# Moving a batch of small matmuls behind the value product, and four tiny steps of a scale chain into PSUM

## Chip, core and metric

One core of a Trainium2 chip. The metric is the device time of one execution in microseconds (us), as the median of several runs. The engines are TensorE (PE; PEld is its weight load), VectorE (DVE), ScalarE (ACT), GpSimd (POOL), and SyncE (SP), which here issues the DMAs. SBUF is the working memory, PSUM holds the results of matmuls in eight banks of 128 partitions by 512 floats.

## What is computed

Two layers over x of shape (4, 1024, 512), with a condition vector of 128 numbers per batch element:

```python
# layer 0: gated feed-forward, FF = 2048, down projection on quantised values
h = x * ((cond @ norm_w.T + 1) * rsqrt(mean(x * x) + 1e-6))
val, gate = split(h @ up_w.T)                    # up_w is (4096, 512)
h = val * gelu(gate)
scale = 127 / clip(max(abs(h), axis=-1), 1e-5)   # one per token
hq = round(h * scale) / scale
x = hq @ ternary(down_w).T + x
# layer 1: adapter whose weights depend on the condition
Wd_b = Wd + 0.1 * (cond @ Wdd.T + bdd)           # Wdd is (65536, 128); the same for Wu_b
x = x + relu(x @ Wd_b.T + bd) @ Wu_b.T + bu
```

The layer-1 weights come from `Wdd` and `Wdu`, two matrices of 65536 x 128 floats that are read from HBM. Everything the kernel does with them besides loading is called the delta work here.

## The kernel before

**Chunks and slots.** The 4096 tokens are handled as 8 chunks c = 0 to 7 of 512 tokens. A chunk has 16 slots j = 0 to 15, one per 128 rows of the feed-forward dimension. Every engine runs its own program of these 128 slots, and semaphores tie them together. There is no planner: the order of work within a slot is written out by hand in each engine's `run(c, par, b)`.

**A slot on PE** (L1302 to L1348) is a gate product (12 matmuls of 128x128 by 128x512, L1176 to L1178, into bank `GATE[j % 2]`), then a value product (12 more, into `VAL[j % 2]`), with other work placed between the two or behind both. In slot 0 of every chunk but the first, `turn_absrun` (L1264) stands between them and `spread_scales` (L1270) behind them. In slots 9 to 12, `down_products` (16 matmuls, L1280, into bank `Y`) multiply the quantised values of the chunk before. `down_products(c, t)` for t > 0 waits for `y_done`, the DVE's `residual` (L968) of row block t - 1, because there is only one bank `Y`. A value product waits for `max_done`: the DVE must have taken the running maximum (L905) of the slot two before, whose bank it reuses.

**A slot on the other engines.** ACT computes gelu of the gate bank (L696), after the DVE's product with the value bank (`h`, L1013) its absolute value into the VAL bank (L710), and in slots 0 to 7 the rounding of the chunk before (`round_pair`, L671 and L674). The DVE runs in this order: `finish_max` and `quantise` (L878) of the chunk before, the running maximum of the slot before (L905), `residual`, `turn_units`, `sum_part` (L909), then `h` (L1013), then the normalisation of the next chunk's x (`scale_x` L855, `x_lower` L860). In slot 0, `turn_units` stands between `finish_max` and `quantise`.

**The delta work.** The upper and lower parts of `Wdd` and `Wdu` go two ways. POOL multiplies, and adds up in two steps, 64 parts (L564, L567, L571), which the DVE finishes (`sum_part`, L909). The rest is 96 units. For each, SP loads two tiles of 128x512 (`load_nat`, L384), the DVE transposes them (`turn_nat`, L895) into one of four places of `natT`. Four units make a batch m, and PE multiplies it with `delta_products(m)`: 16 matmul instructions (32 records in the trace, L1235) into bank `HY`. There is one `natT`: the DVE's first transposes of a batch wait until PE has finished the batch before (`delta_mm`). After every second batch ACT copies `HY` out (`read_sums`, L685), and SP stores it (`store_stage`, L388).

**When units and batches come.** `unit_slots` gives one unit to a slot, two to slots 9 to 12, and leaves one unit out in the slot behind the end of a batch. `batch_at(c, j)` puts a batch's delta products into the slot behind its last unit. So in 18 of 24 cases the slot with the delta products has no unit of its own. In six (slot 10 of chunk 1, slot 11 of chunks 2 to 6) it has one, since one of two is left. The 18 are slots 1, 6 and 13 of chunk 1, slots 2, 7 and 14 of chunk 2, and slots 3, 8 and 14 of chunks 3 to 6. Twelve of these 18 have an odd m, so that `read_sums` and `store_stage` follow: slots 6 and 13 of chunk 1, 7 and 14 of chunk 2, 8 and 14 of chunks 3 to 6.

**From the maximum to the scales.** `finish_max(c)` runs in slot 0 of the next chunk: a reduction of bank `TB` to four numbers per partition (`m4`, L864), a lower bound (`mc`, L866), a reciprocal (`rs`, L868), a product with 127 (`s4`, L870), and a factor for later (`fy`, L871). PE waits for `s4` before `spread_scales` writes it to bank `TB` for the quantisation. The DVE's `mean_square` (L842) is another such small step elsewhere.

**SP's queue** is in order too. In slot j it holds, among others: the transposing loads of the next chunk's x (L344, L349), `load_nat`, `load_part`, loads of x for the residual and stores of x1, and last `store_stage`.

Of the kernel before, what the change touches and what calls it, by code (L numbers as in the profile page):

```python
# [5 lines left out]
F32 = mybir.dt.float32  # L6
# [5 lines left out]
ALU = mybir.AluOpType  # L12
ACT = mybir.ActivationFunctionType
AX = mybir.AxisListType

P = 128
# [9 lines left out]
def conditioned_block(nc, x, cond, norm_w, up_w, down_w, Wd, bd, Wu, bu, Wdd, bdd, Wdu, bdu, out):  # L26
# [6 lines left out]
    NCH = N // CH  # L33
    TT = CH // P
# [19 lines left out]
    with ExitStack() as ctx:  # L54
        def sb(name, shape, dt):
            return ctx.enter_context(nc.sbuf_tensor(name, shape, dt))

        def sem(name):
            return ctx.enter_context(nc.semaphore(name))
# [43 lines left out]
        ss = sb("ss", [P, TT], F32)  # L103
        rstd = sb("rstd", [P, TT], F32)
        mhalf = sb("mhalf", [P, TT], F32)
        m4 = sb("m4", [P, TT], F32)
        mc = sb("mc", [P, TT], F32)
        rs = sb("rs", [P, TT], F32)
        s4 = sb("s4", [P, TT], F32)
        fy = sb("fy", [P, TT], F32)  # L110
        wabs = sb("wabs", [P, 2 * TT], F32)
        unused = sb("unused_gelu", [P, 1], F32)
        wtot = sb("wtot", [P, 4], F32)
# [29 lines left out]
        bank = [ctx.enter_context(nc.psum_tensor(f"bank{i}", [P, 512], F32)) for i in range(8)]  # L143
        GATE, VAL = [bank[0], bank[1]], [bank[2], bank[3]]
        Y, HY, TA, TB = bank[4:8]


        def upn(jj, i):
# [22 lines left out]
        def halves_done(jj, p):  # L171
            return 2 * jj + p + 1 if jj < SPLIT else SPLIT + jj + 1
# [16 lines left out]
        def first_bank(c, k):  # L189
# [32 lines left out]
        absrun_turned, max_read, scale_step, s_turned = (sem(n) for n in (  # L222
            "absrun_turned", "max_read", "scale_step", "s_turned"))
# [39 lines left out]
        def row_in(c, j):  # L263
            return c + 1 < NCH and ((is_first(c) and j == 4) or (c % 2 == 1 and j == 6))
# [19 lines left out]
        def is_first(c):  # L284
            return c == 0
# [23 lines left out]
        def units_at(c, j):  # L309
            return unit_slots.get(FT * c + j, [])  # L310

        def batch_at(c, j):
            return [u // NATT for u in unit_slots.get(FT * c + j - 1, []) if u % NATT == NATT - 1]
# [491 lines left out]
        def _(dve):  # L805
# [54 lines left out]
                dve.tensor_tensor(xn_lo[:, t, :], xn[:, t, :], xn_hi[:, t % 2, :], ALU.subtract).then_inc(x_lo_done, 1)  # L860

            def finish_max(c):
                dve.wait_ge(absrun_turned, c + 1)
                dve.tensor_reduce(m4[:, :], TB[:, :].rearrange("p (t f) -> p t f", t=TT), AX.X, ALU.max).then_inc(max_read, 1)  # L864
                dve.wait_ge(max_read, c + 1)
                dve.tensor_scalar(mc[:, :], m4[:, :], 1e-5, None, ALU.max).then_inc(scale_step, 1)  # L866
                dve.wait_ge(scale_step, 4 * c + 1)
                dve.reciprocal(rs[:, :], mc[:, :]).then_inc(scale_step, 1)  # L868
                dve.wait_ge(scale_step, 4 * c + 2)
                dve.tensor_scalar(s4[:, :], rs[:, :], 127.0, None, ALU.mult).then_inc(scale_step, 1)  # L870
                dve.tensor_scalar(fy[:, :], mc[:, :], wtot[:, 3:4], None, ALU.mult).then_inc(scale_step, 1)  # L871

            def quantise(c, k0):
                if k0 == 0:
# [266 lines left out]
        def _(pe):  # L1141
# [31 lines left out]
            def up_products(par, ft, bank, done):  # L1173
                cols = slice(ft * P, (ft + 1) * P)
                for k in range(KD):
                    pe.matmul(bank[:, :], w_hi[:, k, cols], xh[:, par, k, :], start=(k == 0), stop=False)  # L1176
                    pe.matmul(bank[:, :], w_hi[:, k, cols], xl[:, par, k, :], start=False, stop=False)  # L1177
                    mm = pe.matmul(bank[:, :], w_lo[:, k, cols], xh[:, par, k, :], start=False, stop=(k == KD - 1))  # L1178
                mm.then_inc(done, 1)
# [48 lines left out]
            def delta_products(m):  # L1228
                pe.wait_ge(nat_turned, 8 * m + 8)
                if m % 2 == 0:  # L1230
                    pe.wait_ge(stage_full, m // 2 + 1)
                cols = slice(256 * (m % 2), 256 * (m % 2) + 256)
                for a in range(HB):
                    for t in range(4):
                        mm = pe.matmul(HY[32 * t:32 * t + 32, cols], cond_diag[:, a, :], natT[:, (4 * m + t) % NATT, :, a, :],  # L1235
                                       start=(a == 0), stop=(a == HB - 1))
                mm.then_inc(delta_mm, 1)

            def turn_delta_down(b):
                pe.wait_ge(delta_back[b], 16 * 8)  # L1240
                if b == 0:
                    pe.wait_ge(stage_full, GROUPS + 1)
                    pe.wait_ge(h_scaled, FT * (NCH - 1))
                else:
                    pe.wait_ge(layers_ready, 2 * b - 1)
                for k in range(KD):
                    mm = pe.transpose(HY[:, k * P:(k + 1) * P], delta_d[:, b, k * P:(k + 1) * P], identf[:, :])
                mm.then_inc(delta_turned, 1)
# [8 lines left out]
            def turn_absrun(c):  # L1257
                pe.wait_ge(max_done, FT * (c + 1))
                if c > 0:
                    pe.wait_ge(h_scaled, FT * c)  # L1260
                if c == NCH - 1:
                    pe.wait_ge(layers_ready, 2 * NB)
                for t in range(TT):
                    mm = pe.transpose(TB[:, t * P:(t + 1) * P], absrun[:, t * P:(t + 1) * P], identf[:, :])  # L1264
                mm.then_inc(absrun_turned, 1)

            def spread_scales(c):
                pe.wait_ge(scale_step, 4 * c + 3)
                for t in range(TT):
                    mm = pe.transpose(TB[:, t * P:(t + 1) * P], s4[:, t:t + 1].to_broadcast([P, P]), identf[:, :])  # L1270
                mm.then_inc(s_turned, 1)
# [22 lines left out]
            def run(c, par, b):  # L1294
                first, last = is_first(c), b is None

                if not first:
                    for i in range(2):
                        pe.wait_ge(x_hi_turned[i], 32 * c)
                    pe.wait_ge(x_turned, 16 * TT * c)  # L1300
                    pe.wait_ge(h_done, FT * c - 1)
                for j in range(FT):  # L1302
                    n = FT * c + j
                    if first and j == 0:
                        first_products()
                        continue
                    if first:
                        pe.wait_ge(w_lo_done, halves_done(j, 0))
                    if not (first and j < 2):
                        pe.wait_ge(gelu_done, n - 1)  # L1310
                    up_products(par, FT + j, GATE[j % 2], gate_full)
                    if not first and j == 0:
                        turn_absrun(c - 1)
                    for m in batch_at(c, j):
                        delta_products(m)
                    if last and 10 <= j < 14:
                        turn_delta_down(j - 10)
                    if first and j in (2, 3):
                        if j == 2:
                            pe.wait_ge(base_done, 2)  # L1320
                        pe.wait_ge(ta_freed, TA_BASE + j - 2)
                        for k in range(KD):
                            mm = pe.transpose(TA[:, k * P:(k + 1) * P], base[2 * (j - 2)][:, k * P:(k + 1) * P], identf[:, :])
                        mm.then_inc(ta_full, 1)
                    if first and j + 2 < FT:
                        turn_w(j + 2)
                    if not (first and j < 2):
                        pe.wait_ge(max_done, n - 1)
                    if first:
                        if j < SPLIT:  # L1330
                            pe.wait_ge(w_lo_done, halves_done(j, 1))
                        else:
                            pe.wait_ge(value_turned[j % 2], 32 * ((j - SPLIT) // 2 + 1))
                    up_products(par, j, VAL[j % 2], val_full)
                    if first and j == 8:
                        pe.wait_ge(mean_step, 1)
                        pe.wait_ge(ta_freed, TA_MEAN)
                        pe.matmul(TA[:, 0:1], ones[:, :], wtot[:, 0:1], start=True, stop=True).then_inc(ta_full, 1)
                    if last and 10 <= j < 14:
                        turn_delta_up(j - 10)  # L1340
                    if not first and j == 0:
                        spread_scales(c - 1)
                    if row_in(c, j):
                        spread_row(b)
                    for i in pairs_turned(c, j):
                        turn_pieces(i)
                    if not first and 9 <= j < 9 + TT:
                        down_products(c - 1, j - 9)  # L1348
# [173 lines left out]
```

## Time and profile before

| | us |
|---|---|
| median of 3 runs | 940.36 (938.34 to 940.86) |
| the profiled execution | 937.38 |
| its span, first to last instruction | 935.2 |
| outside the span | 2.2 |
| busy: PE 921.9, PEld 452.1, DVE 687.5, ACT 427.2, POOL 646.0 | |

The span is what the trace covers. A matmul of 512 columns is shown with a length of 0.38 us, though the next one starts 0.216 us later: their ends are modelled and overlap. So a PE pause shows as idle time only where it is longer than that overlap. To find pauses one compares the starts of neighbours. "c6 j14" below is slot 14 of chunk 6.

### The profile page before, as it was taken

The numbers are of one execution on the slowest core, as the hardware profiler recorded it, in microseconds if no ns is written. First come the engines' busy times: TensorE is split into PE (matmuls) and PEld (weight loads), VectorE is DVE, ScalarE is ACT, GpSimd is POOL, SyncE is SP. The second block draws the span as 40 slices with busy tenths as digits, with TensorE's granted clock in tenths as the row PEclk, the third lists the DMA queues.
The fourth block names the chain that finished last, engine by engine and source line by source line (L and its number), as shares of the span: only waits on it lengthen the run. The fifth ranks groups of instructions, "written<-read, shape, count | busy, mean of one in ns | idle before, by whom it ended". The sixth has DMA issues, their size and how long they took to land.

```text
span 935.2 us, 13874 instructions
## 1 busy us (share of the span) xinstructions
PE 921.9 (99%) x5002; PEld 452.1 (48%) x5002; DVE 687.5 (74%) x1034; ACT 427.2 (46%) x788; POOL 646.0 (69%) x565
## 2 busy tenths in 40 slices
PE   9999999999999999999999999999999999999997
PEld 6555544444444444444444444444444444455586
DVE  6778778867878678776878688686878665356676
ACT  7897667214742157123742257222751156215343
POOL 1000049899979998799988999799987999200664
PEclk9999999999999999999999999999999999999999
DMA  9999644655446553574346552584446526020584
GB/s 310 224 229 209 178 138 144 160 156 158 121 133 158 159 152 97 159 196 135 122 121 199 157 161 88 152 212 113 143 116 183 142 68 180 12 74 29 198 296 179
DMA packets 142059, 144.04 MB, mean 154 GB/s; under 512 B 51876, under 2 KB 89256, under 8 KB 141480
## 3 DMA queue, kind: packets, MB, share of 16 engines
q1 hardware_dynamic: 141992, 143.17, 53.7%
q8 instruction: 39, 0.64, 0.3%
q14 instruction: 28, 0.23, 0.1%
HBM read 112.46 MB, written 19.92 MB: 142 GB/s over the span
## 4 chain that ended last, share of the span: by engine, by line
PE 70%; POOL 8%; DVE 7%; issue 5%; DMA 5%; ACT 3%; SPq 2%; DVEq 0%; POOLq 0%; ACTq 0%
PE bank L1176 17%; PE bank L1178 17%; PE bank L1177 17%; POOL delta_reg L564 4%; PE bank L1280 4%; PE bank L1235 4%; DVE delta_reg L895 3%; POOL delta_reg L567 2%; DMA xr<-in_x 2%; DMA delta_reg<-in_L_cond_Wdd 2%; PE bank L1290 1%; POOL delta_reg L571 1%; PE bank L1417 1%; PE bank L1426 1%; PE bank L1447 1%
## 5 line engine op out<-in xcount | busy, mean ns | idle before, releaser
L564 POOL TENSOR_TENSOR delta_reg<-delta_reg,s_bc 128x512 f32<-128x512 f32 x256 | 334.3, 1327 | 91.7 <-DMA delta_reg<-in_L_cond_Wdu 78.7
L1176 PE MATMUL bank<-x_split,w_hi 128*128 128x512 f16 x1016 | 385.3, 379 | 0.9 <-DVE absrun L905 0.9
L1178 PE MATMUL bank<-x_split,w_lo 128*128 128x512 f16 x1016 | 385.1, 379 | 0.0
L1177 PE MATMUL bank<-x_split,w_hi 128*128 128x512 f16 x1016 | 385.1, 379 | 0.0
L710 ACT ACTIVATE bank<-h 128x512 f32<-128x512 f32 x126 | 75.7, 601 | 309.0 <-DVE h L1013 308.9
L895 DVE STREAM_TRANSPOSE delta_reg<-delta_reg 128x512 f32<-128x512 f32 x192 | 197.1, 1107 | 24.6 <-DMA delta_reg<-in_L_cond_Wdd 18.7
L567 POOL TENSOR_TENSOR delta_reg<-delta_reg 128x512 f32<-128x512 f32 x128 | 166.7, 1302 | 10.0
L1013 DVE SCALAR_TENSOR_TENSOR h<-bank,desc,g 128x512 f32<-128x512 f32 x128 | 94.7, 740 | 99.9 <-issue 54.7
L1176 PEld LDWEIGHTS bank<-x_split,w_hi 128*128 128x128 f16 x1016 | 99.4, 98 | 123.0 <-issue 8.2
L1178 PEld LDWEIGHTS bank<-x_split,w_lo 128*128 128x128 f16 x1016 | 99.4, 98 | 119.9
L1177 PEld LDWEIGHTS bank<-x_split,w_hi 128*128 128x128 f16 x1016 | 99.4, 98 | 112.1
L696 ACT ACTIVATE g<-bank,desc 128x512 f32<-128x512 f32 x128 | 87.2, 681 | 90.4 <-PE bank L1178 90.4
L571 POOL TENSOR_TENSOR delta_reg<-delta_reg 128x256 f32<-128x256 f32 x128 | 94.5, 738 | 47.9 <-DVE delta_reg L909 39.0
L1280 PE MATMUL bank<-wqT,qreg 128*128 128x512 fp8e4 x448 | 101.3, 379 | 0.8 <-DVE xr L968 0.8
L905 DVE TENSOR_TENSOR absrun<-bank,absrun 128x512 f32<-128x512 f32 x118 | 80.8, 684 | 21.4 <-ACT bank L710 21.4
L671 ACT ACTIVATE h<-h 128x512 f32<-128x512 f32 x112 | 65.0, 623 | 40.7 <-DVE h L878 40.7
L878 DVE TENSOR_TENSOR h<-h,bank 128x512 f32<-128x512 f32 x112 | 71.4, 678 | 0.6 <-PE bank L1270 0.6
L1280 PEld LDWEIGHTS bank<-wqT,qreg 128*128 128x128 bf16 x448 | 43.6, 98 | 53.7 <-DVE xr L968 2.3
L674 ACT ACTIVATE qreg<-h 128x512 bf16<-128x512 f32 x112 | 63.6, 617 | 0.0
L607 POOL TENSOR_TENSOR out_own<-xn,sc_row 128x512 f32<-128x512 f32 x8 | 10.1, 1290 | 71.9 <-DVE h L1120 69.4
L968 DVE SCALAR_TENSOR_TENSOR xr<-bank,fy,xr 128x512 f32<-128x512 f32 x30 | 22.2, 744 | 39.6 <-issue 27.0
L1235 PE MATMUL bank<-delta_reg,cond_diag 128*32 128x256 f32 x768 | 46.4, 382 | 3.2 <-DVE delta_reg L895 3.1
(182 smaller groups left out, 754.6 us busy)
## 6 DMA issues: line engine op xcount, KB each, us to landing
delta_reg<-in_L_cond_Wdd SPq DMA_DIRECT2D x128, 256.0 KB, 2.9
delta_reg<-in_L_cond_Wdu SPq DMA_DIRECT2D x128, 256.0 KB, 3.2
qreg<-in_L_cond_up_w SPq DMA_DIRECT2D x32, 256.0 KB, 4.7
xr<-in_x SPq DMA_DIRECT2D x30, 256.0 KB, 4.2
x_scratch<-xr SPq DMA_DIRECT2D x30, 256.0 KB, 4.1
xn<-in_x SPq DMA_DIRECT2D x7, 1024.0 KB, 6.1
h<-in_L_cond_down_w SPq DMA_DIRECT2D x4, 1024.0 KB, 7.8
delta_reg<-in_L_cond_down_w SPq DMA_DIRECT2D x8, 512.0 KB, 4.6
```

The lines of the kernel that those rows point to most:

```text
L564: pool.tensor_tensor(part_mul[:, b, :, :], part_w[:, i % 2, :, :], cond_all[:, 2 * pair + b, :].unsqueeze(1).to_broadcast([P, 4, C]), ALU. ...
L567: pool.tensor_tensor(part_mul[:, :, :, 0:64], part_mul[:, :, :, 0:64], part_mul[:, :, :, 64:128], ALU.add).then_inc(part_step, 1)
L571: pool.tensor_tensor(part_low[:, i % 2, 2 * pair:2 * pair + 2, :, :], part_mul[:, :, :, 0:32], part_mul[:, :, :, 32:64], ALU.add).then_inc ...
L696: act.activation(g[:, j % 2, :], GATE[j % 2][:, :], ACT.Gelu, scale=desc[:, 2 * j + 1:2 * j + 2]).then_inc(gelu_done, 1)
L895: dve.transpose(natT[:, t, k, :, :].rearrange("p a (r e) -> p e a r", e=4), nat[:, v % HALVES, :]).then_inc(nat_turned, 1)
L905: dve.tensor_tensor(absrun[:, :], abs_tile(c, j), absrun[:, :], ALU.max).then_inc(max_done, 1)
L1013: dve.scalar_tensor_tensor(h[:, j, :], VAL[j % 2][:, :], desc[:, 2 * j:2 * j + 1], g[:, j % 2, :], ALU.mult, ALU.mult).then_inc(h_done, 1)
L1176: pe.matmul(bank[:, :], w_hi[:, k, cols], xh[:, par, k, :], start=(k == 0), stop=False)
L1177: pe.matmul(bank[:, :], w_hi[:, k, cols], xl[:, par, k, :], start=False, stop=False)
L1178: mm = pe.matmul(bank[:, :], w_lo[:, k, cols], xh[:, par, k, :], start=False, stop=(k == KD - 1))
L1235: mm = pe.matmul(HY[32 * t:32 * t + 32, cols], cond_diag[:, a, :], natT[:, (4 * m + t) % NATT, :, a, :], start=(a == 0), stop=(a == HB - 1))
L1280: mm = pe.matmul(Y[:, :], q[:, f, t * P:(t + 1) * P], wqT[:, f, :], start=(f == 0), stop=(f == FT - 1))
```

## The change

Two things. `m4`, `mc` and `rs` move from SBUF into the first 12 columns of PSUM bank `Y`, except for the last chunk, where a tile in SBUF stays. `s4` and `fy` stay in SBUF. In PE's slot, the delta products go behind the value product (and behind `spread_scales`, ahead of `spread_row`, `turn_pieces` and `down_products`) where the slot has no unit. The six batches in slots with a unit stay between gate and value product.

```diff
-        m4 = sb("m4", [P, TT], F32)
-        mc = sb("mc", [P, TT], F32)
-        rs = sb("rs", [P, TT], F32)
+        scale_tiles = sb("scale_tiles", [P, 3 * TT], F32)
...
+        def scale_tile(c, i):
+            return (scale_tiles if c == NCH - 1 else Y)[:, TT * i:TT * (i + 1)]
...
             def finish_max(c):
+                m4, mc, rs = (scale_tile(c, i) for i in range(3))
                 dve.wait_ge(absrun_turned, c + 1)
-                dve.tensor_reduce(m4[:, :], TB[:, :].rearrange("p (t f) -> p t f", t=TT), AX.X, ALU.max).then_inc(max_read, 1)
+                dve.tensor_reduce(m4, TB[:, :].rearrange("p (t f) -> p t f", t=TT), AX.X, ALU.max).then_inc(max_read, 1)
                 dve.wait_ge(max_read, c + 1)
-                dve.tensor_scalar(mc[:, :], m4[:, :], 1e-5, None, ALU.max).then_inc(scale_step, 1)
+                dve.tensor_scalar(mc, m4, 1e-5, None, ALU.max).then_inc(scale_step, 1)
                 dve.wait_ge(scale_step, 4 * c + 1)
-                dve.reciprocal(rs[:, :], mc[:, :]).then_inc(scale_step, 1)
+                dve.reciprocal(rs, mc).then_inc(scale_step, 1)
                 dve.wait_ge(scale_step, 4 * c + 2)
-                dve.tensor_scalar(s4[:, :], rs[:, :], 127.0, None, ALU.mult).then_inc(scale_step, 1)
-                dve.tensor_scalar(fy[:, :], mc[:, :], wtot[:, 3:4], None, ALU.mult).then_inc(scale_step, 1)
+                dve.tensor_scalar(s4[:, :], rs, 127.0, None, ALU.mult).then_inc(scale_step, 1)
+                dve.tensor_scalar(fy[:, :], mc, wtot[:, 3:4], None, ALU.mult).then_inc(scale_step, 1)
...
                     up_products(par, FT + j, GATE[j % 2], gate_full)
                     if not first and j == 0:
                         turn_absrun(c - 1)
-                    for m in batch_at(c, j):
-                        delta_products(m)
+                    if units_at(c, j):
+                        for m in batch_at(c, j):
+                            delta_products(m)
...
                     if not first and j == 0:
                         spread_scales(c - 1)
+                    if not units_at(c, j):
+                        for m in batch_at(c, j):
+                            delta_products(m)
                     if row_in(c, j):
                         spread_row(b)
```

## Rows read from the trace of the kernel before

**Rows 1.** The page: busy times; then PE's granted clock in 40 slices.
```profile
PE 921.9 (99%) x5002; PEld 452.1 (48%) x5002; DVE 687.5 (74%) x1034; ACT 427.2 (46%) x788; POOL 646.0 (69%) x565
...
PEclk9999999999999999999999999999999999999999
```

**Rows 2.** Waits of PE, whole span: line <- who; us in total, times, longest.
```profile
PE bank L1235 <- DVE delta_reg L895: 3.1, 8, 0.7
...
PE bank L1280 <- DVE xr L968: 0.8, 2, 0.6
...
PE bank L1270 <- DVE s L870: 0.4, 2, 0.3
```

**Rows 3.** Timeline of PE ahead of delta products: start, length; c2 j7, then c6 j14.
```profile
261.99 0.38 PE L1178 MATMUL bank<-x_split,w_lo 128*128 128x512 f16 x1
262.29 0.85 PE L1235 MATMUL bank<-delta_reg,cond_diag 128*32 128x256 f32 x12
...
741.94 0.38 PE L1178 MATMUL bank<-x_split,w_lo 128*128 128x512 f16 x1
742.88 1.93 PE L1235 MATMUL bank<-delta_reg,cond_diag 128*32 128x256 f32 x32 [0.56 <-DVE delta_reg L895]
```

**Rows 4.** Timeline of PE ahead of the spread of scales, c4 j0 and c7 j0.
```profile
437.48 0.38 PE L1177 MATMUL bank<-x_split,w_hi 128*128 128x512 f16 x1
437.70 0.38 PE L1178 MATMUL bank<-x_split,w_lo 128*128 128x512 f16 x1
438.36 0.65 PE L1270 MATMUL bank<-identf,s 128*128 128x128 f32 x4 [0.28 <-DVE s L870]
...
757.93 0.38 PE L1178 MATMUL bank<-x_split,w_lo 128*128 128x512 f16 x1
758.39 0.65 PE L1270 MATMUL bank<-identf,s 128*128 128x128 f32 x4
```

**Rows 5.** Timeline of DVE, `finish_max` in c4 j0.
```profile
435.53 0.69 DVE L864 TENSOR_REDUCE m<-bank 128x4 f32<-128x512 f32 x1 [0.86 <-PE bank L1264]
436.25 1.26 DVE L866 TENSOR_SCALAR mc<-m 128x4 f32<-128x4 f32 x1
...
437.76 0.55 DVE L870 TENSOR_SCALAR s<-rs 128x4 f32<-128x4 f32 x1
```

**Rows 6.** Timeline of POOL beside it.
```profile
436.22 1.27 POOL L567 TENSOR_TENSOR delta_reg<-delta_reg 128x512 f32<-128x512 f32 x1
```

**Rows 7.** Instructions by line: durations ns min/median/max, first and last start us.
```profile
L866 DVE TENSOR_SCALAR mc<-m x8: 169/272/1259, 114.9 to 857.0; 128x4 f32<-128x4 f32 x8
...
L870 DVE TENSOR_SCALAR s<-rs x8: 170/554/1097, 115.3 to 857.4; 128x4 f32<-128x4 f32 x8
```

**Rows 8.** Groups by line, xcount | busy us, mean ns | idle before us.
```profile
L905 DVE TENSOR_TENSOR absrun<-bank,absrun 128x512 f32<-128x512 f32 x118 | 80.8, 684 | 21.4 <-ACT bank L710 21.4
L710 ACT ACTIVATE bank<-h 128x512 f32<-128x512 f32 x126 | 75.7, 601 | 309.0 <-DVE h L1013 308.9
...
L1065 DVE TENSOR_SCALAR sc<-bank 128x16 f32<-128x16 f32 x1 | 0.2, 169 | 0.0
```

**Rows 9.** Timeline of PE, the value product of c1 j3.
```profile
133.72 0.39 PE L1176 MATMUL bank<-x_split,w_hi 128*128 128x512 f16 x1 [0.93 <-DVE absrun L905]
```

**Rows 10.** Timeline of DVE ahead of that.
```profile
130.30 1.57 DVE L886 TENSOR_SCALAR xr<-delta_reg 128x1024 bf16<-128x1024 f32 x1
```

**Rows 11.** Timeline of DVE, c6 j8 and j9.
```profile
697.34 0.75 DVE L1013 SCALAR_TENSOR_TENSOR h<-bank,desc,g 128x512 f32<-128x512 f32 x1 [3.68 <-PE bank L1178]
...
705.70 1.10 DVE L895 STREAM_TRANSPOSE delta_reg<-delta_reg 128x512 f32<-128x512 f32 x1 [2.95 <-DMA delta_reg<-in_L_cond_Wdd]
```

**Rows 12.** Timeline of ACT in c6 j8.
```profile
699.78 0.58 ACT L685 ACTIVATE stage<-bank 128x512 f32<-128x512 f32 x1
```

**Rows 13.** Timeline of SP's issues, c6 j8.
```profile
700.39 0.33 SPq L388 DMA_DIRECT2D delta_scratch<-stage  x1
```

**Rows 14.** Timeline of PE, down products of c6 j10.
```profile
711.69 0.39 PE L1280 MATMUL bank<-wqT,qreg 128*128 128x512 fp8e4 x1 [0.63 <-DVE xr L968]
```

## Prediction

> **What bounds the kernel now.** I read the busy line and the granted clock first: PE is busy 99% of the span at full granted clock, the DVE 74%, POOL 69% [rows 1]. So only three things could shorten the run: less work for PE, a faster PE, or fewer pauses of it. The change keeps every matmul, and the clock has nothing to give. What is left is PE's pauses, and the next view to read is who made PE wait [rows 2]: the delta products waited for the DVE's transposes 8 times, 3.1 us; the spread of the scales for `s4` twice, 0.4 us; the down products for the residual twice, 0.8 us. One value product waited for the running maximum, 0.93 us [rows 9].
>
> These idle times are too small, because a matmul is drawn 0.38 us long while its successor starts earlier. In the timeline I take starts instead. Two neighbouring matmuls of a product start 0.22 us apart [rows 4]. From the last gate matmul to a delta product it takes 0.30 us where nothing is awaited, and 0.94 us in c6 j14, a true pause of 0.64 where the idle column says 0.56 [rows 3]. So I add 0.08 to each pause before delta products, and 0.38 - 0.22 = 0.16 to each pause before the spread or the down products.
>
> **The delta products behind the value product.** Nothing is removed: the same 18 batches of 1.93 us [rows 3] run in the same slot, with one change to and one from this kind of matmul each, as before. What moves is the moment at which the transposes are needed. A value product of 12 matmuls takes 12 x 0.22 = 2.6 us. The longest wait is 0.7 us [rows 2], so the value product covers each of the eight, by at least 1.9 us. The value product itself does not start to wait: the running maximum that it needs stands ahead of the transposes in the DVE's order, one slot before, so where PE now waits for the transposes, that maximum is done.
>
> What is late next? PE arrives earlier at the value product of the slot after next, whose maximum needs the DVE's `h`. In seven of the eight cases the DVE gets there in time: after the last transpose it has a sum, `h`, in slots below 8 the quantisation and the maximum, some 4 us, against 2.6 + 1.9 + 2.6 us of PE. The eighth is c1 j1, 0.7 us. There, the value product of c1 j3 starts at 133.72 after a wait of 0.93 [rows 9], for a DVE that was busy until 131.87 with a step on the pieces of `down_w` that took 1.57 [rows 10]; this chain comes from ACT and hangs on none of PE's products of slot 1. An earlier PE waits 0.7 longer there. That case gives nothing. The others: 3.1 - 0.7 = 2.4, plus 7 x 0.08 = 0.56, together **3.0 us**.
>
> **What the move does to those behind.** `natT` comes free later. After the value product's end the DVE must do `h` (0.75 [rows 11]), ACT the absolute value (0.60), the DVE the maximum (0.68 [rows 8]), 2.0 us and the gaps between them, before it comes to the next transposes; the delta products end about 1.9 us after the value product. Cost 0, with 0.1 to 0.3 us to spare; without that cover it is at most 1.9 us of DVE time per batch, in a DVE that idles 26% of the span. ACT's `read_sums` waits for the delta products, with the next gelu queued behind it, but this gelu needs the next gate product, 2.6 us later. On SP, `store_stage` waits for `read_sums`, and the next slot's transposing load and `load_nat` are queued behind it.
>
> That last queue decides a further gain. In c6 j8, `h` waits for PE until 697.34 after 3.68 us of idleness [rows 11], then come `read_sums` at 699.78 [rows 12], the store at 700.39 [rows 13] with the transposing load and the `load_nat` behind it, and at 705.70 a transpose that waited 2.95 us for its DMA [rows 11]. So the DVE is late in slot 9, and at 711.69 PE has waited 0.63 us for a residual [rows 14]. With the value product ahead of the delta products, `h` of slot 8 comes 1.9 to 2.2 us earlier, the delta products end where the value product ended, at about 697.3, and `read_sums` can start then, more than 2 us before its 699.78. The whole chain up to the residual moves forward by about 2 us, and the pause goes: 0.63 + 0.16 = **0.8 us**. (The other wait of this kind, 0.2, is in chunk 1, with no moved batch near: 0.)
>
> **The scale steps in PSUM.** L866 and L870 work on four numbers and should take 0.17 us, their minimum; their maxima are 1259 and 1097 ns [rows 7]. In c4 j0, L866 starts at 436.25 and ends at 437.51 [rows 5], and POOL's add over SBUF starts at 436.22 and ends at 437.49 [rows 6]: the small step ends when POOL's does. Out of the eight boundaries the seven that change lose up to 2 x 1 us each. A step with PSUM as its source takes 169 ns (L1065 [rows 8]), but with POOL idle then. The Trainium skill, page "SBUF — State Buffer", section "Who interferes with whom", gives the reason: a `tensor_scalar` between SBUF and SBUF uses the port pair that it shares with GpSimd, an exclusive lock; with at most one SBUF operand on its own port it doesn't contend. Rows 5 and 6 agree as to the waiting. Against the change speaks the skill's page "VectorE: DVE Perf Modes", in its section on the TRN2 errata, with a fixed cost of 120 cycles out of PSUM against 58 in SBUF: by that 65 ns more for each step, 0.2 us on the way to `s4`, an estimate, and the sum would be the same.
>
> Writes of the DVE into PSUM have no row. Bounds from rows: 0.17 us as in SBUF, and 0.69 us, the reduction out of PSUM over 512 columns [rows 5]. I take 0.17, by the step of nearest size. Then `s4` comes in c4 at 435.53 + 0.69 + 3 x 0.2 = 436.9 and not 438.3. PE would want it at 437.70 + 0.22 = 437.92, so 1 us remains, and the pause goes: 438.36 - 437.70 - 0.22 = 0.44. In c7 0.46 - 0.22 = 0.24 [rows 4]; the second of the two waits for `s4` in rows 2, in c2, has 0.4 - 0.28 = 0.12 of idleness, plus 0.16: 0.3. Together **1.0 us**. The other 5 us or so that the DVE saves fall where it isn't late for PE, and show nowhere. At the upper bound three steps cost 2.1 us, `s4` comes at 438.4, and this gain is 0.
>
> **The sum.** 3.0 + 0.8 + 1.0 = 4.8 us of PE's pauses. PE has no long wait elsewhere that could take them back [rows 2]; the DVE waits for PE at `h` in every chunk, so that it follows an earlier PE. Against the profiled execution, 937.4 (span 935.2 and 2.2 outside), that is 932.6. That execution lies 3.0 below the median of the runs, 940.36; taking 4.8 from the median gives **935.6 us**.
>
> **Rivals.**
> *Taken back in the same chunk.* In slots 9 to 13 DVE, SP and DMAs work in a chain that wakes PE late even now [rows 14]. If it doesn't follow, the lead from slots 0 to 3 is lost in slot 10 (as c1 j1's is in j3), and the 0.8 isn't won. Then the spread (c7's 0.24) and the delta pauses of slot 14, about 1.4, remain, up to 2 or 3: 937.5 to 939. For it: the 0.6 us waits there. Against: the chain begins with an `h` that waited 3.68 us for PE [rows 11].
> *The change doesn't do what it says in `s4`.* L870 still writes SBUF. If that alone makes it wait, only L866 gets shorter. Even so, in c4 it saves 1.1 us of a pause of 0.44, though POOL may then hold L870 longer: loss up to 1.0, 936.6.
> *Slower.* The mechanism is SP's queue in slot 8: if `store_stage` came later than now, by as much as the batch is moved, 2.2 us, then load, transposes and residual of slots 9 and 10 do too. The pause of slot 10 is already there in c6; taking chunks 3 to 5 to be as close to it, some 4 x 2 = 8 us would be lost and the 4.0 of the other two terms (less c6's 0.8, never won) kept: 940.4 + 8 - 4 = 944. It decides from the point at which `read_sums` starts later than now, that is over 2.5 us after the end of the delta products, as 699.78 stands against 697.3. I see nothing to cause that.
>
> **How the numbers follow.** The forecast (3.8 to 6 us faster) gets 0.62, the rival that takes back 0.18, the one of `s4` 0.06, slower 0.04, no change at all 0.05 (the pauses move to where I don't look), and more than 6 us 0.05 (the DVE's saved time helps further). What a measurement of this kernel can tell from no change is about 0.3%, 2.8 us. Faster than that: 0.62 + 0.06 + 0.05 and a few hundredths of the second case, 0.75. Within it: 0.21. Slower: 0.04. The range runs from 6.5 + 1 of scatter below the median, 932.9, to the less gained of the taken-back case, 939.0.
>
> **What would show it.** Right: no row of PE's waits for L1235 or `s`; L866 and L870 at 0.17 to 0.25 us in chunks 0 to 6, and L870 after the last chunk as before; the pause of c1 j3 grown from 0.93 to about 1.65; in c6 the store of slot 8 at least 2 us nearer to the slot's start. Wrong: new rows of PE waiting for the running maximum or the residual in chunks 2 to 6; transposes that wait for L1235 in most of the slots after a moved batch; a PSUM step over 0.5 us.

## The result: 0.6% faster, and the profile after

| | median us | against the kernel before, interval |
|---|---|---|
| before | 938.18 (7 runs) | |
| after | 932.37 (7 runs) | 0.9938 [0.9921, 0.9955] |

That is 5.8 us (by the interval 4.2 to 7.4), where 4.8 were forecast, and a median 3.2 us below the forecast one, just outside the range that began at 932.9. One of the seven runs of after was slow, 965.8 us at a granted clock of 0.949, and the ratio leaves it out. The profiled execution of after took 932.4, its span is 930.2.

The page of after, busy times:

```profile
PE 921.0 (99%) x5002; PEld 453.6 (49%) x5002; DVE 684.4 (74%) x1034; ACT 429.1 (46%) x788; POOL 645.6 (69%) x565
```

The instruction counts are those of [rows 1], and no engine's busy time differs by more than 3.1 us. The difference is in who made PE wait (columns as in [rows 2]; the lines of PE that matter here are numbered 3 higher than before, those from L1353 on 7 higher):

```profile
PE bank L1360 <- POOL identb L549: 1.9, 1, 1.9
PE bank L1179 <- DVE absrun L908: 1.5, 1, 1.5
PE bank L1463 <- ACT down_hi L782: 0.6, 1, 0.6
PE bank L1159 <- DVE qreg L823: 0.4, 1, 0.4
```

The waits of the delta products (L1235, now L1238), of the spread (L1270, now L1273) and of the down products (L1280, now L1283) in [rows 2] are gone. One wait is longer than in [rows 9], that of the value product in c1 j3, L1179. PE's timeline and the DVE's there:

```profile
132.54 0.38 PE L1181 MATMUL bank<-x_split,w_lo 128*128 128x512 f16 x1
134.40 0.39 PE L1179 MATMUL bank<-x_split,w_hi 128*128 128x512 f16 x1 [1.49 <-DVE absrun L908]
```

```profile
132.47 1.27 DVE L881 TENSOR_TENSOR h<-h,bank 128x512 f32<-128x512 f32 x2
133.67 0.68 DVE L908 TENSOR_TENSOR absrun<-bank,absrun 128x512 f32<-128x512 f32 x1
```

The scale steps, by line (durations min/median/max, then first and last start), against [rows 7]:

```profile
L869 DVE TENSOR_SCALAR bank<-bank x7: 170/171/171, 115.8 to 751.9; 128x4 f32<-128x4 f32 x7
```

```profile
L873 DVE TENSOR_SCALAR s<-bank x7: 161/161/161, 116.2 to 752.3; 128x4 f32<-128x4 f32 x7
L873 DVE TENSOR_SCALAR s<-scale_tiles x1: 170/170/170, 852.5 to 852.5; 128x4 f32<-128x4 f32 x1
```

Maxima of 1259 and 1097 ns have become 171 and 161. And POOL was busy beside most of them. In c4 j0, L869 starts at 435.10, while the first of these was running:

```profile
434.41 0.73 POOL L573 TENSOR_TENSOR delta_reg<-delta_reg 128x256 f32<-128x256 f32 x1
435.22 2.50 POOL L566 TENSOR_TENSOR delta_reg<-delta_reg,s_bc 128x512 f32<-128x512 f32 x2
```

L873 runs at 435.53, in the midst of a POOL product that began at 435.22, and takes 0.16 us.

**A ruler for the traces.** PE's whole steady part lies between the first reduction ahead of the scales and the last. In the trace shown of before these start at 114.2 and 856.3, 742.1 us apart. In after:

```profile
L867 DVE TENSOR_REDUCE bank<-bank x7: 694/700/700, 115.0 to 751.1; 128x4 f32<-128x512 f32 x7
L867 DVE TENSOR_REDUCE scale_tiles<-bank x1: 691/691/691, 851.4 to 851.4; 128x4 f32<-128x512 f32 x1
```

851.4 - 115.0 = 736.4, 5.7 us less. What follows the last reduction is as long in both (78.9 and 78.8 us). I call the stretch between the two reductions the steady part below, and a *pause* the distance between the starts of two neighbouring PE matmuls less what it is where nothing is awaited (0.22, or 0.31 before delta products). Over the steady part, before has pauses of 7.3 us in 17 places, after a single one of 1.65.

### The profile page after: what moved, and what is told of

It reads as the page before. It is cut to its first block, busy times and chain, and to the rows that moved or that the text cites. A ratio compares the mean times of both kernels' runs of the same rounds, so it can differ in the third digit from the quotient of the medians.

```text
span 930.2 us, 13874 instructions
## 1 busy us (share of the span) xinstructions
PE 921.0 (99%) x5002; PEld 453.6 (49%) x5002; DVE 684.4 (74%) x1034; ACT 429.1 (46%) x788; POOL 645.6 (69%) x565
## 4 chain that ended last, share of the span: by engine, by line
PE 94%; ACT 2%; DVE 2%; DMA 1%; issue 1%; SPq 0%; DVEq 0%; ACTq 0%
PE bank L1179 23%; PE bank L1180 23%; PE bank L1181 23%; PE bank L1283 10%; PE bank L1238 5%; PE bank L1293 1%; PE bank L1424 1%; PE bank L1433 1%; PE bank L1159 1%; PE bank L1454 1%; PE bank L1456 1%; PE bank L1455 1%; PE bank L1463 1%; DMA xn<-in_x 1%; PE bank L1464 1%
## 5 line engine op out<-in xcount | busy, mean ns | idle before, releaser
L566 POOL TENSOR_TENSOR delta_reg<-delta_reg,s_bc 128x512 f32<-128x512 f32 x256 | 329.4, 1308 | 90.4 <-DMA delta_reg<-in_L_cond_Wdu 77.2
L1179 PE MATMUL bank<-x_split,w_hi 128*128 128x512 f16 x1016 | 385.3, 379 | 1.5 <-DVE absrun L908 1.5
L1179 PEld LDWEIGHTS bank<-x_split,w_hi 128*128 128x128 f16 x1016 | 99.4, 98 | 123.2 <-issue 9.5
L573 POOL TENSOR_TENSOR delta_reg<-delta_reg 128x256 f32<-128x256 f32 x128 | 98.5, 769 | 43.1 <-DVE delta_reg L912 34.5
L1283 PE MATMUL bank<-wqT,qreg 128*128 128x512 fp8e4 x448 | 101.3, 379 | 0.0
L1283 PEld LDWEIGHTS bank<-wqT,qreg 128*128 128x128 bf16 x448 | 43.9, 98 | 52.2
L1238 PE MATMUL bank<-delta_reg,cond_diag 128*32 128x256 f32 x768 | 46.4, 382 | 0.0
```

The costliest lines, as they stand in the source:

```text
L566: pool.tensor_tensor(part_mul[:, b, :, :], part_w[:, i % 2, :, :], cond_all[:, 2 * pair + b, :].unsqueeze(1).to_broadcast([P, 4, C]), ALU. ...
L573: pool.tensor_tensor(part_low[:, i % 2, 2 * pair:2 * pair + 2, :, :], part_mul[:, :, :, 0:32], part_mul[:, :, :, 32:64], ALU.add).then_inc ...
L1283: mm = pe.matmul(Y[:, :], q[:, f, t * P:(t + 1) * P], wqT[:, f, :], start=(f == 0), stop=(f == FT - 1))
```

## Experiments

The line numbers in the expectations are those of the changed kernel, unless said otherwise.

**e1: the changed kernel again.** No edit.

> The changed kernel once more, on the same chip as its two halves. Theory: it is faster by PE's pauses alone. Compared from the reduction ahead of chunk 0's scales (L864 in the trace of the kernel before, at 114.2) to the one after chunk 7 (856.3), that is 742.1 us before and 736.3 in the first trace of after; expected again 736.3 within 0.2, and the time 5 to 6 us below the kernel before. If the 1 us more than the 4.8 of the forecast was scatter of the start or of the median, the stretch would be 737.3 in a second trace.

931.97 us, ratio 0.9937 [0.9921, 0.9954], 5.9 us below the kernel before by the ratio and 6.5 by the medians; steady part 735.9 (first reduction at 114.4, last at 850.3). So the steady part of the first trace of after was no exception. The 0.2 of tolerance was too tight: the pause of c1 j3 was 1.1 here, and 1.9 in a third trace (e11). It follows the first of the DVE's two long steps in front, L885:

```profile
129.04 0.69 DVE L885 TENSOR_SCALAR delta_reg<-delta_reg 128x1024 f32<-128x1024 f32 x1 [2.36 <-ACT delta_reg L682]
```

```profile
128.66 1.60 DVE L885 TENSOR_SCALAR delta_reg<-delta_reg 128x1024 f32<-128x1024 f32 x1 [2.36 <-ACT delta_reg L682]
```

The first is e1, where POOL was idle at its start, the second e11. In after it took 1.22. Wherever POOL was busy at its start, it ended 0.55 us after POOL's instruction did. The second long step took 1.57 in all three.

**e2: only the move.**

```diff
-            return (scale_tiles if c == NCH - 1 else Y)[:, TT * i:TT * (i + 1)]
+            return scale_tiles[:, TT * i:TT * (i + 1)]
```

> Only the delta products are moved; m4, mc and rs stay in SBUF. Theory (the parts add, each by its own pauses): no pause before delta products, none at the down products, but pauses at the spread of scales stay, some 1.0 to 1.3 us in 3 to 5 of the 7 boundaries, so 1.0 to 1.3 us longer than e1: 4.4 to 4.8 faster than before. Rival (PSUM steps save DVE time that matters further on too): over 2 us longer than e1.

932.68 us, ratio 0.9941 [0.9926, 0.9956], 0.7 us above e1. The steps wait again, and PE with them twice (0.34 us in c2 j0, 0.39 in c5 j0 by starts), not at the boundaries c4 and c7 of [rows 4]:

```profile
L873 DVE TENSOR_SCALAR s<-scale_tiles x8: 169/558/1098, 115.5 to 853.2; 128x4 f32<-128x4 f32 x8
```

```profile
PE bank L1273 <- DVE s L873: 0.4, 2, 0.2
```

So the pauses at the spread come back with SBUF, but in two boundaries and 0.7 us, less than the 1.0 to 1.3 in three to five that I expected: which boundaries lose time changes from execution to execution. The steady part, 737.7, is 1.7 longer than in e1, and 1.0 of that is the pause of c1 j3 (2.14 for 1.13), which varies as much between traces of the changed kernel.

**e3: only the PSUM steps.**

```diff
-                    if units_at(c, j):
-                        for m in batch_at(c, j):
-                            delta_products(m)
+                    for m in batch_at(c, j):
+                        delta_products(m)
...
-                    if not units_at(c, j):
-                        for m in batch_at(c, j):
-                            delta_products(m)
```

> Only the scale steps are in PSUM; all delta products stay between gate and value product. Theory: the spread's pauses go, 1.0 to 1.2 us; the DVE comes 0.6 to 1.5 us earlier to slots 1 to 3 of chunks 2 to 6, so that the pauses before delta products in slots 2 and 3 (0.7, 0.4, 0.3 and 0.4 us in chunks 2, 4, 5, 6) go too, by this half as well: together 2.8 to 3.0 us faster than before. Those of slots 13 and 14 (1.3 us together) and of the down products stay. Rival (the halves share nothing, as the forecast's sum has them): 1.0 us faster, with the pauses of slots 2 and 3 in place.

934.81 us, ratio 0.9966 [0.9951, 0.9982]: 3.2 us faster (by the interval 1.7 to 4.6), which fits the theory's 2.8 to 3.0 and excludes the 1.0 that my sum gave this half. PE's waits for transposes:

```profile
PE bank L1238 <- DVE delta_reg L898: 1.7, 3, 1.0
```

Eight such waits have become three, in c1 j1, c2 j14 and c6 j14. Those of slots 2 and 3 of chunks 2, 4, 5 and 6 went without any batch being moved, because the DVE came out of `finish_max` earlier. At c2 j14 the pause even grew, from 0.25 to 1.05. The transposes there stand behind a residual that waited for its load of x:

```profile
313.78 0.75 DVE L971 SCALAR_TENSOR_TENSOR xr<-bank,fy,xr 128x512 f32<-128x512 f32 x1 [4.01 <-DMA xr<-in_x]
```

The down products kept their pauses, as expected: 1.05 us in c6 j10, 0.20 in c4 j10 and 0.12 in c6 j12.

So the halves give 5.5 and 3.2 alone and 5.9 together (1 minus the ratios of e2, e3 and e1, times 938.5): they cure partly the same pauses.

**e4: the batches of slots 7 and 8 stay.**

```diff
-                    if units_at(c, j):
+                    if units_at(c, j) or j in (7, 8):
...
-                    if not units_at(c, j):
+                    if not (units_at(c, j) or j in (7, 8)):
```

> The changed kernel, but the batches of slots 7 and 8 stay between gate and value product (5 of the 18 moved ones; none of these had a pause of its own). Theory (their move pulls the chain h, read_sums, store, loads, transposes, residual of slots 8 to 10 forward by 2 us): store_stage of c6 j8 comes about 2 us later against the slot's gate product than in the changed kernel, and PE waits for a residual in slot 10 or 11 of some chunks again, 0.1 to 1.0 us in all; 0.3 to 1.0 us longer than e1. Rival (the pause at the down products went for another reason, the scales or the earlier slots 2 and 3): no such wait, the time of e1 within 0.2.

935.06 us, ratio 0.9951 [0.9933, 0.9969], against 0.9937 for e1. The intervals overlap, so the times don't settle this; the traces have to. The down products wait again:

```profile
PE bank L1283 <- DVE xr L971: 0.5, 2, 0.3
```

By starts these are pauses of 0.28 us in c4 j10 and 0.49 in c6 j10, and a third of 0.36 in c1 j12, 1.1 together. SP's issues of c6 j8, in e4 and then in after:

```profile
699.95 0.33 SPq L390 DMA_DIRECT2D delta_scratch<-stage  x1
700.32 1.21 SPq L346 DMA_TRANSPOSE x_split<-xn_hi  x1
```

```profile
695.02 0.33 SPq L390 DMA_DIRECT2D delta_scratch<-stage  x1
695.39 1.21 SPq L346 DMA_TRANSPOSE x_split<-xn_hi  x1
```

and PE's delta products of this slot, first e4, then after:

```profile
691.97 1.93 PE L1238 MATMUL bank<-delta_reg,cond_diag 128*32 128x256 f32 x32
```

```profile
692.02 1.93 PE L1238 MATMUL bank<-delta_reg,cond_diag 128*32 128x256 f32 x32
```

In e4 a value product of 2.6 us still follows them, so the slot ends at 696.4, and the store comes 3.5 us behind its end. In after the slot ends with them at 693.9, and the store comes 1.1 us behind. So the chain of the forecast runs 2.4 us earlier in its slot. The pauses of c4 j10 and c6 j10 stand in all three traces of before (0.9 to 1.2 us together), in e3 (1.25) and here (0.8), and in none of the nine traces in which the batches of slots 7 and 8 are behind: a batch that never had a pause of its own cures another one. (The two profiled executions lie 4.0 apart: 1.0 of it are the pauses of the down products, 1.1 is c1 j3, 2.2 against 1.1, and 2.0 lie ahead of the first reduction, 116.4 against 114.4.)

**e5: all 24 batches behind.** The six whose slot has a unit move as well.

```diff
-                    if units_at(c, j):
-                        for m in batch_at(c, j):
-                            delta_products(m)
...
-                    if not units_at(c, j):
-                        for m in batch_at(c, j):
-                            delta_products(m)
+                    for m in batch_at(c, j):
+                        delta_products(m)
```

> The changed kernel with the six remaining batches (slot 10 of chunk 1, 11 of chunks 2 to 6), whose slot has a unit, behind the value product as well. Theory: the DVE's transpose of that slot stands ahead of its h and now waits for delta products that end 2.6 us later; it idles up to 2 us more in each of the six, in the slots in which the DVE is the late one; PE waits for it at the residuals of slots 12 and 13 for up to 1 us each: 1 to 6 us longer than the changed kernel. Rival (DMAs set the pace of slots 9 to 13 and hide it): within 0.5 us of the changed kernel.

936.47 us, ratio 0.9974 [0.996, 0.9987], 4.1 to 4.5 us above after and e1 by the medians, 3.4 by the ratios: six batches give back most of what 18 have won. The DVE's waits for the delta products, then PE's for the residual:

```profile
DVE delta_reg L898 <- PE bank L1238: 21.7, 6, 5.2
```

```profile
PE bank L1283 <- DVE xr L971: 3.0, 4, 1.2
```

There are exactly six waits of the DVE, and by starts PE pauses in slot 12 of all six chunks, 0.92, 0.88, 1.37, 0.54, 0.26 and 0.23 us, 4.2 together. The DVE waits up to 5.2 us, not 2: its chain in slots 9 to 13 runs ahead by then, so that it comes early and waits for the value product of 2.6 us as well, and at most for part of the gate product. (In after there are such waits as well, 7.2 us in five cases, all in slots whose batch stayed; none costs PE anything.) This is a slower case that I hadn't among my rivals, and the condition in the change is what keeps it off.

This trace shows one thing more, in c1 j3. After the pause of 2.15 us, eight matmuls of the value product start 0.43 us apart where 0.22 is usual:

```profile
137.88 0.63 PE L1179 MATMUL bank<-x_split,w_hi 128*128 128x512 f16 x1
138.31 0.63 PE L1180 MATMUL bank<-x_split,w_hi 128*128 128x512 f16 x1
```

The granted clock of the stretch from 136.6 to 139.5 is 0.50, that is the lower level, 1.2 GHz; it cost 1.7 us. In e8 the same follows a pause of 2.20. In e2, e4 and e7 it does not, after 2.12 to 2.18, nor in any trace with a shorter pause. So the pause of c1 j3, which the change makes longer, had a second cost in two traces. Whether the untraced runs with a mean clock of 0.998 (933.9 of after, 934.8 of e1) owe their length to it isn't shown; none of the 39 runs of before in the comparisons is below 0.999.

**e6: the last piece of down_w two slots later**, on top of the change.

```diff
-            return [i for i, slot in enumerate((9, 10, 11, 12, 13, 14, 15, 17)) if slot == FT * c + j]
+            return [i for i, slot in enumerate((9, 10, 11, 12, 13, 14, 15, 19)) if slot == FT * c + j]
...
-            return [i for i, slot in enumerate((10, 11, 12, 13, 14, 15, 16, 20)) if slot == FT * c + j]
+            return [i for i, slot in enumerate((10, 11, 12, 13, 14, 15, 16, 21)) if slot == FT * c + j]
```

> The changed kernel with the last eighth of down_w quantised in slot 3 of chunk 1 and not in slot 1 (and turned in slot 5, not 4). Theory (the pause that slot 1's delta products hand on to the value product of c1 j3, 1.65 us by starts, comes from ACT's and DVE's two long steps on that piece, which wait for POOL): the pause goes or falls below 0.5, and the time by 1.1 to 1.65 us against the changed kernel: 7 us faster than the kernel before. Rival (the DVE is late in chunk 1 anyway, for the first quantisations): the pause moves to slot 5 or so, no gain.

930.55 us, ratio 0.9916 [0.99, 0.9931], 7.9 us faster than before. The steady part is 850.1 - 115.4 = 734.7:

```profile
L867 DVE TENSOR_REDUCE bank<-bank x7: 690/700/700, 115.4 to 749.8; 128x4 f32<-128x512 f32 x7
L867 DVE TENSOR_REDUCE scale_tiles<-bank x1: 691/691/691, 850.1 to 850.1; 128x4 f32<-128x512 f32 x1
```

No pause is left in it. So the pause of c1 j3 came from that piece, and what c1 j1 handed on was to be had after all.

**e7: only m4 in PSUM.**

```diff
-            return (scale_tiles if c == NCH - 1 else Y)[:, TT * i:TT * (i + 1)]
+            return (scale_tiles if c == NCH - 1 or i > 0 else Y)[:, TT * i:TT * (i + 1)]
```

> The changed kernel with only m4 in PSUM, mc and rs in SBUF: L869 reads PSUM and writes SBUF, L873 reads and writes SBUF. Theory (a tensor_scalar waits for POOL only if both its tensors are in SBUF): L869 takes 0.16 to 0.18 us in every chunk, L873 waits as before, 0.5 to 1.1 us in most of chunks 1 to 6. Rival (it is the write to SBUF that waits): L869 waits as well, up to 1.2 us.

By line, L869 (PSUM to SBUF in seven chunks), then L873 (SBUF to SBUF in all):

```profile
L869 DVE TENSOR_SCALAR scale_tiles<-bank x7: 160/161/162, 115.1 to 751.7; 128x4 f32<-128x4 f32 x7
```

```profile
L873 DVE TENSOR_SCALAR s<-scale_tiles x8: 169/330/1065, 115.5 to 852.3; 128x4 f32<-128x4 f32 x8
```

The time was 932.14 us (one run), no pause at the spread. Four of the seven L869 ran wholly inside a POOL instruction. So a source in PSUM suffices; the write to SBUF doesn't wait. My rival about `s4` falls with this, and with L873 in after. The step for `fy`, L874, SBUF to SBUF with a column as factor, waited here twice, for 1.3 us, where I had thought that it never would:

```profile
436.22 1.31 DVE L874 TENSOR_SCALAR fy<-scale_tiles,wtot 128x4 f32<-128x4 f32 x1
```

**e8: a column as factor.**

```diff
-                dve.tensor_scalar(ss[:, :], ss[:, :], 1.0 / D, EPS, ALU.mult, ALU.add).then_inc(ms_done, 1)
+                dve.tensor_scalar(ss[:, :], ss[:, :], inv_d[:, 0:1], EPS, ALU.mult, ALU.add).then_inc(ms_done, 1)
```

> The changed kernel; mean_square (L844, in SBUF) takes its factor from a column in SBUF instead of a constant. It took 1.1 to 1.3 us in chunks 1 to 6, where fy's step, which has such a column, never took more than 0.23 while between SBUF tiles. Theory A (fy's step only never waited because it followed directly on a step that had waited): still 1.1 to 1.3 us. Theory B (with a column as factor the step doesn't need what POOL holds): 0.22 us in every chunk. Either way no change in time beyond 0.3 us, since the DVE isn't late in slot 5.

```profile
L846 DVE TENSOR_SCALAR ss<-ss,inv_d x7: 230/1020/1277, 49.2 to 679.5; 128x4 f32<-128x4 f32 x7
```

932.84 us (one run, with the stretch at half rate named in e5). It waits all the same, so theory B falls: a column as factor doesn't help. But theory A's reason doesn't hold either. In e7 `fy`'s step followed directly on one that had waited and still took 1.3 us, in the two chunks in which POOL's next instruction began 0.02 us after it; where it took 0.22 in the kernel before, that came 0.14 us after it.

**e9 and e10: the kernel before, traced twice more.**

> The kernel before, unchanged, for a second trace of it. Theory (PE's pauses hang on where POOL stands when a short DVE step begins, so they differ from one execution to the next): the floor of a chunk between pauses is the same (105.4 or 105.9 us from one reduction of L864 to the next, less chunk 1), but single pauses differ by up to 1 us from the first trace, and their sum, 7.3 us there, is another by 0.5 to 2 us. Rival (fixed pauses): the same pauses within 0.1 us each, and the scatter of the runs comes from the first 114 us.

> A third trace of the kernel before; the same expectations as for e9. By the theory the sums of the pauses of the three traces differ by over 0.5 us and the first 114 us by 1 to 3 us; by the rival only the latter.

The steady parts, by the reduction of e9 and then of e10, are 740.5 and 739.9 us:

```profile
L864 DVE TENSOR_REDUCE m<-bank x8: 686/692/693, 114.7 to 855.2; 128x4 f32<-128x512 f32 x8
```

```profile
L864 DVE TENSOR_REDUCE m<-bank x8: 684/692/692, 113.9 to 853.8; 128x4 f32<-128x512 f32 x8
```

PE's pauses come to 5.7 and 5.2 us, not 7.3, with another distribution: those of c1 j1 (0.78, 0.69) and c2 j2 (0.71, 0.62) stay, the one of c4 j0 (0.45 in [rows 4]) is missing in both, the one of c6 j10 is 1.13 and 0.92 for 0.79. The first 114 us vary by 0.8. So the pauses are not fixed, and the start scatters by less than the 1 to 3 us that I expected. For the spread the traces show the link with POOL: in c4, L866 and L870 together took 1.81 us in the first trace, with the pause, and 1.07 and 1.22 in e9 and e10, without. For the other pauses the link is argued. The trace on which I built had the largest pauses of three.

**e11 and e12: the changed kernel and e6's on one chip.**

> The changed kernel beside the one with the late piece, on one chip. 1.1 to 2.2 us longer than e12, all of it the pause of the value product of c1 j3.

> The kernel of e6 again. If its 7.9 us against the kernel before hold: 930 to 931 us, no pause of PE over 0.1 us between the first and the last reduction ahead of the scales, 734.7 us apart within 0.2.

931.36 (0.9916 [0.9894, 0.9938]) and 930.94 us (0.9909 [0.9883, 0.9936]). The steady parts differ as expected (736.6 and 735.0; 1.92 us in c1 j3 against nothing there, though 0.29 in c1 j12), the medians only by 0.4, and the two profiled executions not at all (931.8 and 931.7), because e12's first reduction came at 115.7 and e11's at 114.2. The first reductions lie between 113.9 and 114.7 in the three traces of before and between 113.6 and 116.4 in those of the changed kernel and its variants. That e6's edit saves 1.0 to 1.9 us of the steady part is shown (736.4, 735.9 and 736.6 against 734.7 and 735.0); that its median is lower is within the scatter on this chip (1.4 us lower over e1 and e6, 0.4 here).

## Why the prediction was wrong in the number and right in most of its reasons

The forecast missed the median by 3.2 us: 935.6 against 932.4. Two parts:

**The base, 2.2 us.** The step that failed is "taking 4.8 from the median". I took the sum from 940.36, the median of three runs. With four more it was 938.18, and in the later comparisons 938.5 (19 runs), 938.7 (13) and 939.3 (7). The profiled execution, 937.4, was the better base; with it the same sum would have given 932.6. That this meets 932.4 is luck: the base would have been 0.8 too low and the sum 1.0 too small. I allowed 1 us of scatter at the lower end, for three runs that lay 2.5 us apart. This alone put 932.37 outside the range.

**The sum, 1.0 us: 4.8 for 5.8.** Term by term, from the first trace of each kernel:

- *Delta products, 3.0.* The pauses before them were 3.9 by starts and are 0; c1 j3 took back 0.56 (1.09 to 1.65). So 3.3. The forecast counted eight waits of the idle column and missed two below its resolution. Its point on c1 j1, that an earlier PE waits longer in j3 and that the case gives nothing, was right in kind: e6 shows that the long DVE step in front was the cause. It expected "about 1.65" of a column that showed 0.93 before; that column shows 1.49, and 1.65 is the pause by starts. It is a coincidence in any case: e1, e11, e2 and e4 have 1.1, 1.9, 2.1 and 2.2.
- *Down products, 0.8.* 1.3: c4 j10 (0.13) and c1 j12 (0.36) went too. I had put the latter at 0, "with no moved batch near", in after it is gone, in e1 0.11 and in e4 back at 0.36. It scatters, whatever the kernel: 0.29 in e12, and none in e9 and e10. So the 0.36 isn't shown to be the change's doing; the 0.9 of c4 and c6 is (e4).
- *Scales, 1.0.* Right by the first traces, and about 0.15 more inside the three spreads that waited (the sum to `s4` in c4 is 436.8, printed as 436.9). In e9 and e10 the pauses of this term are 0.4 and 0.1. But e2 and e3 show that the term is not this half's own worth, which is 0.4 to 0.7 beside the other half (by the ratios, by the medians) and 3.2 without it. "The other 5 us or so that the DVE saves ... show nowhere" was wrong for this half by itself: the saved time also cures the pauses of slots 2 and 3.

These make 3.3 + 1.3 + 1.15 = 5.7, the difference of the steady parts. Against the three traces of before (740.8 on average) and of after (736.3) it would be 4.5. The two late traces of before, at 936.3 and 934.9 us, lie below all seven runs beside them (936.6 to 941.5). So 4.5 us of the measured 5.8 to 7.9 are located in PE's pauses, and where the other 1.3 to 3.4 lie stays open: in the traces it is neither the start nor the end, and the longer runs of before have no trace.

**The other points.** *Cost 0 of the later `natT`:* right, the DVE waits for delta products in no slot behind a moved batch; but the bound without that cover, "at most 1.9 us of DVE time per batch", doesn't hold where the slot has a unit: in e5 such a wait took up to 5.2. *The chain of slot 8:* right, 2.4 us for "about 2" (e4). *The steps in PSUM:* 0.16 to 0.17 us, the value taken; the upper bound of 0.69 was far off. *The rivals:* the lead was not taken back in slots 9 to 13, since the chain there moved along; `s4` doesn't wait (e7); the slower case through `store_stage` did not come, the store being earlier, not later. There is a slower case, e5's, which the change avoids; I should have priced it, since the condition `units_at` in the diff points at it. "The clock has nothing to give" left out that it can take: e5 and e8 lost 1.7 us to it behind the longer pause of c1 j3.

## What to carry to other kernels

Where PE is 99% busy, look for its pauses by the distance of starts, and let PE do first the work that doesn't have to wait. Check that no other engine has a wait for the postponed work queued ahead of what PE needs from it next: the same edit gains in 18 slots and loses in six. Don't add up two halves of a change before asking whether they cure the same pause. And take the base of a forecast from as many runs as there are, with their spread in the range: here it cost 2.2 us, and the sum 1.0.

## What the runs showed of the hardware

- A `tensor_scalar` of four numbers on the DVE from SBUF to SBUF takes 0.17 us or up to 1.31; wherever it was drawn out, it ended 23 to 29 ns after a POOL instruction did. The Trainium skill, page "SBUF — State Buffer", section "Who interferes with whom", says that this form of instruction can contend for a port pair with GpSimd and that the later one waits, and the traces agree. It holds for a constant and for a column as factor (e7, e8). With the source in PSUM it takes 0.16 us to SBUF and 0.17 to PSUM, whatever POOL does (e7 and after).
- The reciprocal of four numbers never waited, not even between two tiles in SBUF: 177 to 179 ns in all 24 cases of the three traces of before, many of them wholly inside a POOL instruction. So of the steps that the change takes out of SBUF only the two `tensor_scalar` gained by it.
- The fixed cost out of PSUM that I had quoted from the Trainium skill, page "VectorE: DVE Perf Modes", isn't seen: 161 ns from PSUM against 170 in SBUF. Only the write to PSUM costs something on other steps: the reduction 700 ns for 692, and the reciprocal 191 in seven chunks against 178 in the last, where it stays in SBUF:

```profile
L871 DVE RECIPROCAL bank<-bank x7: 191/191/192, 116.0 to 752.1; 128x4 f32<-128x4 f32 x7
L871 DVE RECIPROCAL scale_tiles<-scale_tiles x1: 178/178/178, 852.3 to 852.3; 128x4 f32<-128x4 f32 x1
```

- Pauses of PE change size and place between executions of one kernel: 5.2 to 7.3 us in three traces of the same program.
- The granted clock can fall for a few matmuls behind a short pause: to 0.50 for 2.9 us behind pauses of 2.15 and 2.20 us (e5, e8), and not behind 2.18 (e4).
